# A state-space block with a quantised gate: softplus in phases, x_proj turned round, low-rank products on three row groups, dtx on VectorE

## The reference, cut to what matters

```python
xn = _layernorm(x)                                    # x: 2 x 1024 x 512, float32
# the scan branch, DIN = 1024 channels, N = 16 states, R = 32
x, z = split(xn @ in_proj_w)
xc   = silu(conv_b + sum_k conv_w[k] * shift(x, k))   # 4 taps over time
ssm_p = einsum('bdl,ed->ble', xc, x_proj_w)           # 64 = R + 2N values a step
dt_r, Bm, Cm = rmsnorm of the three parts of ssm_p
dt = softplus(einsum('blr,dr->bdl', dt_r, dt_proj_w) + dt_bias)
h  = exp(dt*A) * h + dt * Bm * xc                     # scan over 1024 steps
s  = ((einsum(h, Cm) + D*xc) * silu(z)) @ out_proj_w.T
# the gate branch: three linears with 4-bit weights and a rank-32 correction
w = (q - 7.5) * (scale * 0.005)[:, None]
y = x @ w.T + 0.02 * (x @ A @ Bm)                     # gate, up, down
g = silu(down(silu(gate(xn)) * up(xn)))
out = x + s * g
```

## Time and profile before

| | before |
|---|---|
| median of three runs | 1401.92 us |
| profiled execution | 1404.62 us, span 1402.8 us |
| busy in the span | PE 86%, DVE 74%, POOL 54%, ACT 52% |
| conv stage and norms, image 0 | 24 to 157 us |
| softplus stage, image 0, h = 0 and h = 1 | 157 to 210 us, 413 to 471 us |
| conv stage and norms, image 1 | 737 to 821 us |
| softplus stage, image 1, h = 0 and h = 1 | 821 to 873 us, 1080 to 1136 us |
| output stage, image 0 and 1 | 683 to 737 us, 1348 us to the end |

### The profile page before, as it was taken

How to read it: one execution, slowest core, us unless ns; L and a number is a source line. 1 busy time by engine, 2 the same in 40 slices (tenths; PEclk the granted TensorE clock), 3 DMA queues, 4 the chain that set the end, 5 groups by cost and what they waited for, 6 DMA issues and landing times.

```text
span 1402.8 us, 13293 instructions
## 1 busy us (share of the span) xinstructions
PE 1200.2 (86%) x4598; PEld 658.4 (47%) x4598; DVE 1036.0 (74%) x827; ACT 732.9 (52%) x892; POOL 762.7 (54%) x418
## 2 busy tenths in 40 slices
PE   4999828889988688999999982888998778899998
PEld 3664415445543344555444541454554334455543
DVE  2866478989948989997425537989984899899740
ACT  2111566667638566774012266666763856677400
POOL 1000048889923688895130005888982378889511
PEclk9779879999998899999999986999999989999999
DMA  6542114989961188898811111588986118889860
GB/s 210 202 138 85 41 58 106 219 197 218 232 160 60 60 211 205 196 226 195 311 39 38 45 46 51 126 208 206 223 214 156 60 60 216 207 194 223 195 231 37
DMA packets 60612, 214.08 MB, mean 153 GB/s; under 512 B 6362, under 2 KB 6490, under 8 KB 60132
## 3 DMA queue, kind: packets, MB, share of 16 engines
q0 software_dynamic: 16128, 88.09, 32.2%
q1 hardware_dynamic: 42836, 119.50, 24.6%
q10 hardware_dynamic: 1584, 5.68, 1.0%
HBM read 102.18 MB, written 22.98 MB: 89 GB/s over the span
## 4 chain that ended last, share of the span: by engine, by line
PE 30%; POOL 27%; DVE 18%; DMA 9%; issue 8%; ACT 6%; SPq 1%; POOLq 0%; DVEq 0%; ACTq 0%
POOL ub L529 25%; DVE hb L1103 10%; PE psA L747 9%; PE psM L947 7%; DMA bn<-ss_rows_scratch 4%; PE psM L773 3%; DVE th L972 2%; DMA dt<-w_out_dram 2%; PE psM L794 2%; PE psT L870 2%; POOL yT L540 2%; DMA yT<-yc 2%; PE psA L843 1%; DVE hb L972 1%; DVE yT L972 1%
## 5 line engine op out<-in xcount | busy, mean ns | idle before, releaser
L529 POOL TENSOR_TENSOR ub<-dtx,bn 128x1024 f32<-128x1024 f32 x256 | 625.1, 2456 | 115.4 <-DVE hb L1103 101.3
L1103 DVE TENSOR_TENSOR_SCAN hb<-psA,ub 128x1024 f32<-128x1024 f32 x256 | 584.7, 2285 | 70.9 <-ACT psA L646 64.2
L870 PE MATMUL psT<-ident,hb 128*128 128x128 f32 x2048 | 275.1, 277 | 135.0 <-DVE yT L972 76.0
L870 PEld LDWEIGHTS psT<-ident,hb 128*128 128x128 f32 x2048 | 232.4, 142 | 302.0 <-issue 125.6
L773 PE MATMUL psM<-xnT,w_ts 128*126 128x512 f32 x704 | 345.1, 622 | 30.0 <-DVE hid L972 22.1
L665 ACT ACTIVATE yc<-psT,ssm 128x512 f32<-128x512 f32 x336 | 219.0, 685 | 214.6 <-PE psT L870 214.4
L646 ACT ACTIVATE psA<-dt,cc 128x1024 f32<-128x1024 f32 x256 | 285.6, 1116 | 35.5 <-DVE hb L1103 35.5
L522 POOL TENSOR_TENSOR dtx<-dt,xc 128x1024 f32<-128x1024 f32 x12 | 28.2, 2353 | 362.1 <-DVE dt L1087 362.1
L773 PEld LDWEIGHTS psM<-xnT,w_ts 128*126 128x126 f32 x704 | 128.5, 199 | 148.6 <-issue 123.0
L892 PE MATMUL psM<-w_dn,hid 126*128 126x512 f32 x352 | 165.0, 597 | 0.0
L972 DVE SCALAR_TENSOR_TENSOR yT<-psT,ssm,yT 128x512 f32<-128x512 f32 x144 | 104.9, 735 | 33.2 <-DMA yT<-yc 31.9
(11 more groups left out here) (88 smaller groups left out, 807.7 us busy)
## 6 DMA issues: line engine op xcount, KB each, us to landing
yT<-yc POOLq DMA_DIRECT2D x112, 768.0 KB, 6.5
bn<-ss_rows_scratch SPq DMA_DIRECT2D x64, 512.0 KB, 4.9
w_ts<-w_gu_scratch SPq DMA_DIRECT2D x44, 504.0 KB, 3.4
w_ts<-w_in_dram SPq DMA_DIRECT2D x32, 256.0 KB, 3.5
z_scratch<-th SPq DMA_DIRECT2D x32, 256.0 KB, 5.8
hb<-z_scratch SPq DMA_DIRECT2D x16, 512.0 KB, 9.1
w_gu_scratch<-hid ACTq DMA_DIRECT2D x11, 504.0 KB, 3.2
yT<-x_dram SPq DMA_DIRECT2D x2, 2048.0 KB, 12.5
```

What stands on the lines that cost most here:

```text
L529: pool.tensor_tensor(ub[:, i % 2, :], dtx[:, i, :], bn[:, t, :], ALU.mult).then_inc(s_u, 1)
L870: mm = pe.transpose(psT[:, at % 2, i * P:(i + 1) * P], hb[:, t * DH + i, tb * P:(tb + 1) * P], ident[:, :])
L1103: dve.tensor_tensor_scan(hb[:, t * DH + i, :], psA[:, i % 2, :], ub[:, i % 2, :], 0.0, ALU.mult, ALU.add).then_inc(s_scan, 1)
```

## The change

Four parts, in the order of the diff.

1. **Weights.** The 22 items become 11 tiles j, each with gate, up and down together, spread over the eight blocks by `prepared(m)` (1, 1, 2, 1, 1, 2, 1 and 2 tiles). The rank-32 operands of gate, up and down lie on partitions 0-31, 32-63 and 64-95, and gate and up products alternate on TensorE.
2. **x_proj turned round.** The weights `wx` are now the stationary side and `xc` the moving one: two matmuls of 512 columns a block, with 64 output rows each, in place of eight of 64 columns. The sum then has to be copied by ScalarE (`xr`) and turned by four transposes.
3. **Softplus in phases.** ScalarE does Abs and Relu for all four blocks, then Exp and 1 + Exp for all four, then the four Ln. The temporary `e` lies in `dtx[i]`, `w` in four different buffers. In h = 1 the gate products of TensorE stand behind all `turn_back`s.
4. **dtx on VectorE**, for all four blocks (`drive`); GpSimd keeps the inputs only.

```diff
-PT = 3
+def prepared(m):
+    return range(IT * m // DB, IT * (m + 1) // DB)
...
         def soft_tmp(i):
-            return (hb[:, DH, :], hb[:, DH + 3, :]) if i % 2 else (ub[:, 0, :], ub[:, 1, :])
+            return dtx[:, i, :], [ub[:, 0, :], ub[:, 1, :], hb[:, DH, :], hb[:, DH + 3, :]][i]
...  (GpSimd)
-                    for i in range(DH - 1):
-                        k = blk(b, h, i)
-                        pool.wait_ge(s_dt, k + 1)
-                        pool.tensor_tensor(dtx[:, i, :], dt[:, i, :], xc[:, h * DH + i, :],
-                                           ALU.mult).then_inc(s_dtxp, 1)
...
                     for i in range(DH):
-                        if i == DH - 1:
-                            pool.wait_ge(s_dtx, b * HALVES + h + 1)
+                        pool.wait_ge(s_dtx, blk(b, h, i) + 1)
                         input(0, 0, i)
...  (ScalarE)
-                        it = PT * m + j
-                        if b == 0 and it < IT:
-                            act.wait_ge(s_lrr, 2 * it + 5)
-                            act.dma_start(w_gu[it], wf[:, it % QD, :]).then_inc(s_wst[it % QD], 16)
+                    if b == 0:
+                        for j in prepared(m):
+                            act.wait_ge(s_lrr, 3 * j + 5)
+                            act.dma_start(w_gu[j], wf[:, j % QD, :]).then_inc(s_wst[j % QD], 16)
...
                 act.wait_ge(s_xp, b + 1)
+                act.activation(xr, psM[:, 0, :], ACT.Copy).then_inc(s_xr, 1)
+                v = psT[:, 0, :].rearrange("p (a c e) -> p c a e", c=2, e=E)
+                act.wait_ge(s_xt, b + 1)
                 act.activation(sq, v, ACT.Square).then_inc(s_sq, 1)
...
                     for i in range(DH):
-                        if i == 0 and h == 0:
-                            ahead(0)
                         relu_abs(i)
-                        if i == 3:
+                    for i in range(DH):
+                        one_plus_exp(i)
+                        if i == 0:
+                            ahead(1 - h)
+                        if i == (2 if h else DH - 1):
                             ahead(2 - h)
-                        if i:
-                            log(i - 1)
-                        one_plus_exp(i)
-                        if i == 1:
-                            ahead(1 - h)
+                    for i in range(DH):
+                        log(i)
...  (TensorE)
+            def low_rank(j):
+                pe.wait_ge(s_lrr, 3 * j + 3)
+                at = slice(j * IM, (j + 1) * IM)
+                for k in range(HK):
+                    for gu in range(2):
+                        rows = slice(gu * R, (gu + 1) * R)
+                        mm = pe.matmul(lr_bank(gu)[:, k * IM:(k + 1) * IM], la[rows, k * P:(k + 1) * P],
+                                       lb[rows, at], start=True, stop=True)
...
-                    for tb in range(TB):
-                        mm = pe.matmul(psM[:, 0, tb * E:(tb + 1) * E], xc[:, k, tb * P:(tb + 1) * P], wx[:, k, :],
-                                       start=(k == 0 and tb == 0), stop=(k == DB - 1 and tb == TB - 1))
+                    for c in range(2):
+                        mm = pe.matmul(psM[c * E:(c + 1) * E, 0, :], wx[:, k, :], xc[:, k, c * CH:(c + 1) * CH],
+                                       start=(k == 0), stop=(k == DB - 1))
...
-                pe.wait_ge(s_xpr, b + 1)
+                pe.wait_ge(s_xr, b + 1)
+                for a in range(JD):
+                    mm = pe.transpose(psT[:, 0, a * P:(a + 1) * P], xr[:, a * P:(a + 1) * P], ident[:, :])
+                mm.then_inc(s_xt, 1)
...
                     dt_proj(0)
                     dt_proj(1)
+                    for i in range(2):
+                        if h:
+                            turn_back(i)
+                        else:
+                            gate_up(b, 0, 0, 0, 2 + i, landed(b, w_half(0, 0)))
+                        dt_proj(2 + i)
...  (VectorE)
+                    def drive(i):
+                        softplus(i)
+                        dve.wait_ge(s_dt, blk(b, h, i) + 1)
+                        dve.tensor_tensor(dtx[:, i, :], dt[:, i, :], xc[:, h * DH + i, :], ALU.mult).then_inc(s_dtx, 1)
+                    if h:
+                        for i in range(DH):
+                            finish_y(i)
...
+                    lost(0)
+                    silu_gate(1 - h, 1 - h)
+                    lost(1)
+                    lost(2)
+                    hidden(1 - h, 1 - h)
+                    silu_gate(2 - h, h)
+                    lost(3)
+                    drive(0)
                     if h:
                         hidden(1, 1)
+                    drive(1)
+                    drive(2)
+                    scan(0, 0, 0)
+                    drive(3)
                     scan(0, 0, 1)
```

More of the change, by code:

```diff
@@ L222, in build @@
         s_xp = sem("s_xp")
+        s_xr = sem("s_xr")
+        s_xt = sem("s_xt")
         s_xpr = sem("s_xpr")
@@ L803, in _ @@
                 if b == 0:
-                    for use in range(3):
-                        low_rank(use)
+                    low_rank(0)
                 for m in range(DB):
@@ new lines, in add_low_rank @@
+            def add_low_rank(j):
+                dve.wait_ge(s_deq, 2 * j + 2 + QD)
+                for gu in range(2):
+                    w = wf[:, j % QD, gu * HK * IM:(gu + 1) * HK * IM]
+                    dve.wait_ge(s_lr, 3 * j + gu + 1)
+                    stt(w, lr_bank(gu)[:, 0:HK * IM], LR_SCALE, w, ALU.mult, ALU.add).then_inc(s_lrr, 1)
+                w = w_dn[0:IM, j, :]
+                dve.wait_ge(s_lr, 3 * j + 3)
+                stt(w, lr_bank(2)[0:IM, :], LR_SCALE, w, ALU.mult, ALU.add).then_inc(s_lrr, 1)
```

182 lines of the change are left out of this document (66 added, 116 removed).

## The result

The changed kernel takes 1409.62 us (median of 20 runs, 1398.69 to 1425.15); the kernel before took 1402.02 beside it (20 runs, 1396.73 to 1405.25). The ratio is 1.0047, with a 95% interval from 1.0031 to 1.0062: slower by 7.6 us, where 28.5 were forecast. The direction was right, the size was not, and the runs of the changed kernel scatter three times as widely as those before. (The ratio leaves out the two executions with the lowest granted clock, 1422.65 us at 0.928 and 1425.15 us at 0.924; the median of the other 18 is 1409.1.)

The account below looks back on a forecast made before the run. TensorE's queue was taken to bound image 0's conv stage, a chain between engines the softplus stages. Terms -4 + 1.5 + 5.7 + 5.3 + 12 + 8 = +28.5 on 1404.6 gave 1433.1, median 1430.4; forecast 1418 to 1444, range 1405 to 1448.

Parts of the forecast that it names:

- -4 for image 0 and +1.5 for image 1: Conv stages: predicted change in us for each image, with ends -12 and +2.3 for image 0, -2 and +2.5 for image 1.
- signs of being wrong: Listed beforehand: VectorE operations of 1.23 beside GpSimd, a tile clearly under 2.9 us, image 0's Square before 140.
- Eleven tiles 32 us, before as after.: Image 0's conv stage: rank-32 matmuls stay the same in number, 2.9 us a tile on TensorE, so no saving.
- 1411 to 1416: Rival case: full clock in image 0's conv stage and concurrent row groups, with the forecast's own softplus terms; chance 0.18.
- So the turning saves nothing in the stream: Conv stages: turned x_proj costs 1.8 us a block on TensorE, against 1.89 before.
- at most 0.45 a block less: Image 1's conv stage: saving if x_proj's two 64-row halves ran side by side, -3.6 us in all.
- 8.5 us a projection: Image 0's conv stage: cost on TensorE of each of the seven projections after the first.
- its end for the full clock, -12: Image 0's conv stage: the same sum at 7.1 us a projection and 1.85 an x_proj part.
- The tail of 20.7 us: Image 0's conv stage: time from the last projection's end to the Square, 10.9 us before the change.
- Softplus, h = 0, +5.7 and +5.3.: Softplus stages of images 0 and 1: longer because VectorE, sharing with GpSimd, has everything before it; ends +2 and +8.5.
- Softplus, h = 1, +12 and +8.: Softplus stages of images 0 and 1: longer as ScalarE waits for gate products behind the turn_backs; ends +6 and +14.
- Ln 3 does not end the stage: Softplus: the forecast had VectorE end it; the rival that Ln 3 does gave 1378 us, chance 0.08.

Follow-up runs that it names:

- the conv part alone: Kernel before with only the conv-stage changes (spread low-rank tiles on three row groups, x_proj turned, Copy and transposes), old softplus and dtx: 1382.1 us, ratio 0.9848.
- the softplus part: Kernel before with only the softplus phases, dtx on VectorE and the TensorE and VectorE orders that go with them: 1443.07 us, ratio 1.0278.
- taking two of the three out of the exclusion: Changed kernel with one operand of VectorE's add and of its dtx product read from PSUM instead of SBUF: 1387.83 us.
- the Tanh moved behind: Changed kernel with h = 1's first gate Tanh behind the fourth 1 + Exp, the second behind the first decay: 1396.68 us, ratio 0.9953.
- the low-rank part alone: Kernel before with only the low-rank tiles spread over the stage on three row groups; x_proj, softplus and dtx as before: 1388.42 us, ratio 0.991.
- four the fastest: Changed kernel with softplus in two pairs of blocks, gate Tanh behind, hidden(0) and a piece of the up product moved later: 1373.19 us, ratio 0.9787.

## Why the prediction was wrong in size

The step that failed is the conv stage: its terms priced the low-rank tiles and the two halves of x_proj as matmuls in series. The sum had -4 for image 0 and +1.5 for image 1; the conv part alone measures -20.9. That is 18.4 of the 20.9 us by which the forecast missed. (Taken in the other order, behind the softplus part, the conv part is worth 1409.6 - 1443.1 = -33.5 and the softplus part its +40 where the sum had 31: the two are not independent, but the conv terms are the larger miss either way.) Two of the prediction's own signs of being wrong came true: a tile in 1.6 us, and the Square before 140, at 130.98.

The last projection of image 0 was forecast to end at 131.2 and ended at 112.4. Of these 18.8 us the eight tiles behind the first are 9 (14.2 us for 23.2), the seven projections 6, the five x_proj parts 6 (6.5 us for 12.5), the first projection with its tile 1; TensorE's waits for VectorE take 4 back (6.1 us for 2.2). Point by point:

- *"Eleven tiles 32 us, before as after."* Wrong: 1.6 us a tile at the full clock, by row groups side by side; on one row group a tile takes 2.9 again and the kernel 13.7 us more. I had the rule before me and left it out since no row of before shows two row groups at once. But that kernel reads all its low-rank operands from one row group, so it could not have shown it. The prediction gave this case 0.18 with "1411 to 1416", and the kernel came out just below.
- *"So the turning saves nothing in the stream"*, -2 to +2.5 for image 1. Wrong for the same reason: two matmuls on different halves of the columns run side by side, 1.08 us a block in place of 1.89; the turned x_proj alone gives 14.6. The end of the range that did have them side by side, "at most 0.45 a block less", was mis-sized too: it is 0.81.
- *8.5 us a projection.* Mis-sized: most ran at the full 7.13, 60.5 us for all eight where before had 69.0. The prediction expected "some of the low clock" to go; 8.5 of the 12.0 us that eight projections took over the full-clock time went. Even its end for the full clock, -12, kept the serial tiles and so lay too near.
- *The tail of 20.7 us, with the last tile ahead of the last x_proj parts:* right, 18.6. Since TensorE is early, it is VectorE's adding that it waits for there (7.33 us).
- *Softplus, h = 0, +5.7 and +5.3.* Right in mechanism and size: the gap from first Abs to the first scan of n = 1 grew by 6.5, and in (1, 0) by 4.8. VectorE's three operations a block, with the add at 3.25 beside GpSimd, are the path; taking two of the three out of the exclusion gives 21.8 us. The price of the low level was too small: "up to 3.4" for a dt_proj, where it takes 3.78.
- *Softplus, h = 1, +12 and +8.* Right in mechanism, 3 and 1 us too large: ScalarE waits 6.64 and 2.20 us for gate products in (0, 1), the gaps grew by 8.7 and 6.9, and the Tanh moved behind gives 12.9 back. What I missed is that the sum has two prices for one text: 27.5 us on the new conv stage (1409.6 - 1382.1), 40 on the old one.
- *Ln 3 does not end the stage:* right. All Ln are through 5.5 us earlier and none of it arrives.

So the changed kernel is slower although its conv part is a gain of 20.9: the phases put all of ScalarE's Exp work ahead of the first Ln, VectorE's 30 us behind it, and TensorE's dt_proj, turn-backs and gate products in series ahead of both. The old order had those beside each other.

Open: what decides at which level TensorE runs in the softplus stages (the same instructions ran at either in different kernels); why the two conv parts add up to 20.9 and not 29.2, beyond 2.3 us of waits; and that the old softplus stages, unchanged, came out 6 us shorter in all in the kernels with x_proj or the low-rank part alone than in the profile of before.

## What to carry to other kernels

Fewer table loads save time only where ScalarE ends the stage; first ask what starts when the last phase begins, and what that engine needs from there. Here, from first Abs to first scan of n = 1 in (0, 0), two loads gave the slowest stage (58.0 us), four the fastest (45.6), eight lay between (51.6). A trace in which all small matmuls use one row group says nothing about what several would do: where the change makes a thing possible that the old kernel couldn't show, its price belongs into the sum at both ends, not outside it. A chain laid through TensorE in short pieces inherits its clock, and here with it a wider scatter (26.5 us against 8.5).

## What the hardware showed that I had not expected

- fp32 products of 32 rows by 126 columns on two row groups start 0.01 us apart, and a third group's product of 512 columns joins them: a tile in 1.6 us, on one row group 2.9. Two products onto different 64 columns of the array, 512 columns of data each, take 1.08 us together and 1.93 on the same ones (at the full clock).
- VectorE operations with one operand in PSUM took 1.22 beside GpSimd's products, those with both in SBUF up to 3.25; with both in SBUF the two engines take turns, whole instructions at a time, and the pair costs the sum of the two alone, to within 0.2 us.
- The same dt_proj took 1.98 or 3.78 us in the same place of the program, by TensorE's level; where it is on the path, twenty runs of one kernel spread over 26 us, the shorter the higher their mean granted clock (0.924 to 0.947, correlation -0.96).
